# Cross-attention with a quantised feed-forward: another order of work in the prologue and the query phase

## The reference

```python
def attn(Q, K, V, WQ, WK, WV, WO, mask):          # 16 heads of 64
    Qh, Kh, Vh = (einsum('btd,hdk->bhtk', a, w) for a, w in ((Q, WQ), (K, WK), (V, WV)))
    logits = einsum('bhtk,bhsk->bhts', Qh, Kh) / sqrt(64) + mask * -1e9
    A = einsum('bhts,bhsv->bhtv', softmax(logits), Vh)
    return concat_heads(A) @ WO
def ffn(x, W1, b1, W2, b2):                        # 1024 hidden, quantised with the range of the whole tensor
    return qlinear(gelu(qlinear(x, W1, b1)), W2, b2)
x = x + attn(layernorm(x), ctx, ctx, WQ, WK, WV, WO, mask)
x = x + ffn(layernorm(x), W1, b1, W2, b2)
```

## Time and profile before

| | |
|---|---|
| median of three runs | 1099.45 us (1097.84 to 1099.54) |
| the profiled execution | 1099.71 us, of which its span 1097.6 us |
| TensorE busy | 1025.7 us (93%) |
| VectorE, ScalarE, GpSimd busy | 938.5 us (85%), 855.1 us (78%), 767.9 us (70%) |
| mean granted TensorE clock | 0.991 of full speed |
| first query product of TensorE | 19.47 us after the span's start |
| first key product | 98.08 us |

### The profile page before, as it was taken

The page is one execution under the profiler, slowest core; times in us unless marked ns, Lnnn a source line. Parts: engine busy times, 40 slices in busy tenths (PEclk is TensorE's granted clock), DMA queues, the critical chain, the costliest instruction groups (busy, mean ns, idle before and its releaser), DMA issues.

```text
span 1097.6 us, 37623 instructions
## 1 busy us (share of the span) xinstructions
PE 1025.7 (93%) x10639; PEld 643.8 (59%) x10639; DVE 938.5 (85%) x2668; ACT 855.1 (78%) x1809; POOL 767.9 (70%) x1106
## 2 busy tenths in 40 slices
PE   3999999999999999999999999999999999997728
PEld 2555566666666666666666666666666666665317
DVE  5776888888888888888888888888888888886997
ACT  3665888888888888888888888888888888886906
POOL 2337777777777777777777777777777777774800
PEclk9999999999999999999999999999999999999969
DMA  8400776666666666666666666666666666664003
GB/s 243 132 1 14 133 134 134 135 138 138 138 138 138 134 134 134 137 138 135 134 135 136 135 134 135 136 138 134 132 134 136 138 138 135 134 134 140 1 0 120
DMA packets 435436, 136.75 MB, mean 125 GB/s; under 512 B 407666, under 2 KB 434390, under 8 KB 435414
## 3 DMA queue, kind: packets, MB, share of 16 engines
q1 hardware_dynamic: 435414, 136.47, 59.5%
HBM read 28.60 MB, written 6.55 MB: 32 GB/s over the span
## 4 chain that ended last, share of the span: by engine, by line
PE 64%; DVE 13%; issue 10%; ACT 9%; DVEq 2%; DMA 2%; ACTq 1%; POOL 1%; SPq 0%; POOLq 0%
PE front L368 16%; PE front L370 14%; PE front L369 14%; PE back L1309 8%; PE front L1287 5%; PE tp L1287 4%; ACT prob L742 3%; DVE k_l L1039 3%; DVE hrange L1138 3%; DVE hrange L1139 3%; DVE prob L985 2%; ACT q_h L796 2%; ACT k_h L752 1%; DVEq L374 1%; ACT ctx_h L792 1%
## 5 line engine op out<-in xcount | busy, mean ns | idle before, releaser
L616 POOL TENSOR_TENSOR hl<-prob,hl 100x361 f16<-100x361 f32 x511 | 430.7, 855 | 67.7 <-ACT hl L748 39.9
L742 ACT ACTIVATE prob<-prob,nmax 100x361 f32<-100x361 f32 x512 | 293.9, 587 | 39.0 <-DVE nmax L985 38.9
L1309 PEld LDWEIGHTS back<-v,pT 128*128 128x128 f16 (+1 forms) x4608 | 163.9, 97 | 39.7 <-issue 9.3
L748 ACT ACTIVATE hl<-prob 100x361 f16<-100x361 f32 x352 | 176.1, 500 | 7.9
L1039 DVE SCALAR_TENSOR_TENSOR k_l<-front,k_h 128x362 f16<-128x362 f32 x256 | 136.3, 532 | 48.1 <-ACT k_h L752 45.5
L1309 PE MATMUL back<-v,pT 128*128 128x65 f16 (+1 forms) x4608 | 172.8, 193 | 1.4 <-DMA pT<-hl 1.4
L368 PE MATMUL front<-ctx_h,wk_h 128*128 128x362 f16 x512 | 164.3, 321 | 5.4 <-issue 0.8
L370 PE MATMUL front<-ctx_h,wk_l 128*128 128x362 f16 x512 | 161.8, 316 | 0.0
L369 PE MATMUL front<-ctx_l,wk_h 128*128 128x362 f16 x512 | 161.5, 315 | 0.0
L756 ACT ACTIVATE v<-front 128x512 f16<-128x512 f32 (+1 forms) x192 | 113.9, 594 | 52.6 <-PE front L370 52.6
L368 PE MATMUL front<-wv_h,ctx_h 128*128 128x512 f16 (+1 forms) x384 | 146.3, 381 | 9.3 <-DVE k_l L1039 9.3
(11 more groups left out here) (206 smaller groups left out, 2047.6 us busy)
## 6 DMA issues: line engine op xcount, KB each, us to landing
ctx_raw<-ctxT SPq DMA_DIRECT2D x33, 361.0 KB, 3.1
pT<-hl SPq DMA_TRANSPOSE x253, 3.6
xs<-x SPq DMA_DIRECT2D x8, 400.0 KB
q_all<-x SPq DMA_DIRECT2D x32, 100.0 KB
out<-q_all SPq DMA_DIRECT2D x32, 100.0 KB
xb<-out SPq DMA_DIRECT2D x5, 640.0 KB, 8.3
out<-xb SPq DMA_DIRECT2D x25, 128.0 KB, 1.8
q_all<-wq SPq DMA_DIRECT2D x1, 1024.0 KB, 6.5
```

The lines of the kernel that those rows point to most:

```text
L616: pool.tensor_tensor(hl[0:T, n % RT, 1, 0:S], prob[0:T, n % RP, 0:S], hl[0:T, n % RT, 0, 0:S], ALU.subtract).then_inc(s_lo, 1)
L742: act.activation(prob[0:T, n % RP, 0:S], prob[0:T, n % RP, 0:S], ACT.Exp, bias=nmax[0:T, n:n + 1], scale=-1.0).then_inc(s_exp, 1)
L748: act.activation(hl[0:T, h % RT, 0, 0:S], prob[0:T, h % RP, 0:S], ACT.Copy).then_inc(s_ha, 1)
L1309: ins = pe.matmul(obank[j % 2][:, n % GH * DV:(n % GH + 1) * DV], pT[0:r, n % RT, part_ * ST + st, :], v2[half][0:r, st, v, n % HT, :], st ...
```

## The change

The change has four parts.

1. **Moments.** For chunks 0 and 1 VectorE uses one aggregate instruction per item and two small steps (`pair_x`) in place of the eight steps of `ln_moments`; for chunk 1 this work moves from GpSimd to VectorE.
2. **Prologue order.** VectorE takes the maxima of weight 0 before the statistics of chunk 1, which now stand behind `x_low(0, 0)` and `low_w(0, 0)`; the statistics of chunk 2 move into chunk 0. ScalarE's `norm_x(1, 1)` moves from the prologue to a place behind the first copy of chunk 0. TensorE multiplies the fp16 identity with itself, in two halves of 64 columns, 120 times from the start and 36 times behind the transposes of chunk 0 (`warm_up`); `top_w(0)` now stands before these transposes. The first two query tiles are made in another order: all eight products that need only the weights' high part first, then the four with the low part (`first_two`).
3. **ScalarE in each chunk.** The second half of `high_w` stands behind the second copy, before `x_high`. `norm_x` of the chunk after next is cut in two halves, one before and one after the last copy.
4. **First keys.** TensorE's wait for both banks and for the zeroed pads goes. The first two jobs of the first turn wait for the last copy of their own bank, and the wait for the pads stands before the first product of queries and keys (QP).

```diff
--- before.py
+++ after.py
@@ -203,6 +203,7 @@
     stats = place("stats", [P, B, 6], F32)
     mean = place("mean", [P, B], F32)
     var = place("var", [P, B], F32)
+    pair = place("pair", [P, 2 * TB, 2], F32)
     rstd = place("rstd", [P, B], F32)
     shift = place("shift", [P, B], F32)
     lnt = place("lnt", [P, 4, B], F32)
@@ -564,8 +565,8 @@
         link = chain(pool, s_lp)
         for c in range(NB):
             bs = slice(c * TB, (c + 1) * TB)
-            if c == 0:
-                pool.wait_ge(s_lv, 8)
+            if c < 2:
+                pool.wait_ge(s_lv, (TB + 2) * (c + 1))
             else:
                 pool.wait_ge(s_st, TB * (c + 1))
                 ln_moments(link, pool, c)
@@ -683,14 +684,15 @@
             act.activation(part_w((wq_h, wk_h, wv_h, wo_h)[n], n, half), part_w(raws[n], n, half), ACT.Identity,
                            scale=winv[:, n:n + 1]).then_inc(s_whi, 1)
 
-        def norm_x(c, par):
+        def norm_x(c, par, items=range(TB)):
 
             act.wait_ge(s_rs, c + 1)
-            for i in range(TB):
+            for i in items:
                 b = c * TB + i
                 ins = act.activation(xn[0:T, par, i, :], xs[0:T, b, :], ACT.Identity, scale=rstd[0:T, b:b + 1],
                                      bias=shift[0:T, b:b + 1])
-            ins.then_inc(s_xn, 1)
+            if items[-1] == TB - 1:
+                ins.then_inc(s_xn, 1)
 
         def x_high(c, par):
 
@@ -706,25 +708,28 @@
         def q_chunk(c, par, more=True):
             split = (c - 1 if 2 <= c <= 4 else None)
             q_out(c, 0)
+            if c == 0:
+                norm_x(1, 1)
             if split:
                 high_w(split, 0)
             q_out(c, 2)
+            if split:
+                high_w(split, 1)
             if more:
                 x_high(c + 1, 1 - par)
             q_out(c, 4)
             if c + 2 < NB:
-                norm_x(c + 2, par)
+                norm_x(c + 2, par, range(TB // 2))
             if c == NB - 2:
                 act.wait_ge(s_msk, 16)
                 act.activation(mask_b[0:T, 0:S], mask_b[0:T, 0:S], ACT.Copy, scale=-1.0e9).then_inc(s_mb, 1)
-            if split:
-                high_w(split, 1)
             q_out(c, 6)
+            if c + 2 < NB:
+                norm_x(c + 2, par, range(TB // 2, TB))
         norm_x(0, 0)
         x_high(0, 0)
         high_w(0, 0)
         high_w(0, 1)
-        norm_x(1, 1)
         for c in range(NB - 1):
             if c == NB - 2:
                 act.wait_ge(s_wlo, 8)
@@ -912,6 +917,8 @@
         def q_chunk(c, par, more=2):
 
             q_out(c, 1)
+            if c == 0:
+                stats_x(2)
             if c < 3:
                 abs_w(c + 1, 0)
             elif c < 6:
@@ -948,18 +955,26 @@
                 ctx_unit(0)
                 dve.scalar_tensor_tensor(out=wconst[:, 1:2], in0=wunit[:, 2:3], scalar=1.0 / VS, in1=wunit[:, 3:4],
                                          op0=ALU.mult, op1=ALU.mult).then_inc(s_wc, 1)
+        def pair_x(c):
+
+            bs = slice(c * TB, (c + 1) * TB)
+            dve.wait_ge(s_st, TB * (c + 1))
+            for b in range(c * TB, (c + 1) * TB):
+                dve.bn_aggr(pair[0:T, b, :], stats[0:T, b, :]).then_inc(s_lv, 1)
+            dve.wait_ge(s_lv, (TB + 2) * c + TB)
+            dve.tensor_scalar(var[0:T, bs], pair[0:T, bs, 1], EPS, None, ALU.add).then_inc(s_lv, 1)
+            dve.tensor_scalar(mean[0:T, bs], pair[0:T, bs, 0], -1.0, None, ALU.mult).then_inc(s_lv, 1)
         stats_x(0)
-        dve.wait_ge(s_st, TB)
-        ln_moments(chain(dve, s_lv), dve, 0)
-        stats_x(1)
+        pair_x(0)
         abs_w(0, 0)
         abs_w(0, 1)
         unit_w(0)
-        low_w(0, 0)
         start(dve, (s_k, s_v, s_cm, s_cr, s_sv, s_max, s_mg, s_hv, s_ri, s_nrm, s_x1, s_ln))
         x_low(0, 0)
+        low_w(0, 0)
+        stats_x(1)
+        pair_x(1)
         low_w(0, 1)
-        stats_x(2)
         for c in range(NB):
             if c == NB - 2:
                 dve.wait_ge(s_wlo, 8)
@@ -1212,8 +1227,25 @@
             wait(pe, s_cm, a + 1)
             pe.transpose(ps[:, 512 - P:512], cmax[:, 0:1].broadcast_to([P, P]), ident[:, :]).then_inc(s_ct, 1)
 
+        def first_two():
+
+            pe.wait_ge(s_whi, 1)
+            for m in range(2):
+                for k in range(KD):
+                    for t, x_ in enumerate((xnT_h, xnT_l)):
+                        pe.matmul(proj[m][:, 0:TW], wq_h[:, k, m * P:(m + 1) * P], x_[:, 0, k, :],
+                                  start=k == 0 and t == 0, stop=False)
+            pe.wait_ge(s_wlo, 1)
+            for m in range(2):
+                for k in range(KD):
+                    ins = pe.matmul(proj[m][:, 0:TW], wq_l[:, k, m * P:(m + 1) * P], xnT_h[:, 0, k, :],
+                                    start=False, stop=k == KD - 1)
+                ins.then_inc(s_qp, 1)
+
         def q_chunk(c, par, more=True):
             wait(pe, s_xtl, KD * (c + 1))
+            if c == 0:
+                first_two()
             for m in range(NM):
                 if m == NM // 2 and more:
                     x_transposes(c + 1, 1 - par)
@@ -1224,21 +1256,29 @@
                 if m == NM // 2 and c == NB - 1:
                     top_f()
                 wait(pe, s_qe[m % 2], NM // 2 * c + m // 2)
-                if c == 0 and m % (NM // 2) == 0:
-                    pe.wait_ge(s_wlo, m // (NM // 2) + 1)
+                if c == 0 and m < 2:
+                    continue
+                if c == 0 and m == NM // 2:
+                    pe.wait_ge(s_wlo, 2)
                 for k in range(KD):
                     ms = slice(m * P, (m + 1) * P)
                     ins = split3(pe, proj[m % 2][:, 0:TW], (wq_h[:, k, ms], wq_l[:, k, ms]),
                                  (xnT_h[:, par, k, :], xnT_l[:, par, k, :]), k == 0, k == KD - 1)
                 ins.then_inc(s_qp, 1)
+        def warm_up(times):
+
+            for _ in range(times):
+                for h in range(2):
+                    pe.matmul(tp[1][h * DK:(h + 1) * DK, 0:T], identb[:, h * DK:(h + 1) * DK], identb[:, 0:T],
+                              start=True, stop=True)
+
+        warm_up(120)
+        top_w(0)
         x_transposes(0, 0)
-        top_w(0)
+        warm_up(36)
         for c in range(NB):
             q_chunk(c, c % 2, c < NB - 1)
 
-
-        phase1_over(pe)
-        wait(pe, s_zero, PADS)
 
         def bank_read(kind, n, a):
 
@@ -1257,6 +1297,8 @@
                 a, ps = b + later, banks.get((kind, n))
                 if ps is not None:
                     g = jobs.index((kind, n, later))
+                    if part == "first" and g < 2:
+                        wait(pe, s_qe[g], NB * NM // 2)
                     if g >= 2 or part != "first":
                         had = (before + jobs)[g]
                         bank_read(had[0], had[1], b + had[2])
@@ -1277,6 +1319,8 @@
                                      (wv_h[:, k, hs], wv_l[:, k, hs]), k == 0, k == KD - 1)
                     ins.then_inc(s_vp, 1)
                 elif kind == "QP":
+                    if part == "first" and n == 0:
+                        wait(pe, s_zero, PADS)
                     if n % (NP_ // 2) == 0:
                         wait(pe, s_q, 2 * a + n // (NP_ // 2) + 1)
                     wait(pe, s_k, NP_ * a + n + 1)
```

## The result

The changed kernel takes 1092.83 us (median of 5 runs, 1091.09 to 1094.62); the kernel before takes 1098.49 beside it (5 runs, 1097.84 to 1099.54). The ratio is 0.9948, with a 95% interval of 0.9933 to 0.9963: faster by 5.7 us.

What follows compares the result with a forecast made beforehand. Bounds: the first 20 us, where TensorE waits behind VectorE's order and starts at half clock, and gaps in the query phase. Terms 4.5+2.6+0.7 = 7.8 us, taken from the profiled 1099.71, gave 1091.9; range 1090.3 to 1096.5.

Steps and rivals of the forecast that it cites:

- the item loop starts less than 7 us earlier: Sign, at the loop behind the query phase, that would show the prediction wrong.
- The pair's price: Prologue: two identity products on the two column halves cost 60 ns at full clock, between 44 and 88.
- one after the other: Rival, prologue: column halves do not run together; top_w(0) at 14.8, gain 4.2 us, 1095.5; chance 0.14.
- The narrow loads: Rival, prologue: each narrow load also waits for the product before it; 172 ns a pair, 1105.6 us; chance 0.06.
- The estimate made from this rule, 190 ns: Identity pair's cost by the skill's load-overlap rule, result over 1105; the prediction held that the trace disagrees.
- The first term: Prologue up to chunk 1's transposes: they begin at 21.15 instead of 25.66, 4.5 us gained.
- the hole before m=3: Chunk 0: TensorE stands still some 2.5 us; VectorE's queued work holds m=3 until about 19.4.
- GpSimd and ScalarE's start 1.35 later at 19.05: Chunk 1's normalisation: after VectorE's moments end at 17.7, norm_x(1) starts at 19.05 and takes 2.07 us.
- The second term: Query phase: ScalarE's new order removes its stops at chunk starts 3 to 5, 2.6 us gained.
- the new waits for VectorE: Query phase: VectorE's q_out copies then hold TensorE 0.25 us in chunks 3 and 4, 0.33 before chunk 5.
- The third: First keys: K0 starts 0.93 us earlier, but K2 near 99.7 instead of 100.40; 0.7 us gained.
- The clock: Rival: identity products do not raise it, 1097.3 us, or it falls in chunk 0's hole, 1094.0; chance 0.11.

Runs made afterwards that it cites:

- e7: Changed kernel with both products of each identity pair on the same column half of the array: 1096.14 us.
- e4: Changed kernel with VectorE's second low_w of weight 0 moved behind the statistics of chunk 2: 1091.98 us.
- e2: Changed kernel with only ScalarE's order in a chunk put back as in the kernel before: 1096.03 us.
- e12: The changed kernel run again without any edit: 1094.19 us, ratio 0.9954 to the kernel before.
- e11: Changed kernel with the first two query tiles made in the old order, the first product waiting for low_w(0, 0): 1093.03 us.
- e3: Changed kernel with TensorE's wait for both banks and the pads put back ahead of the first keys: 1094.85 us.
- e1: Changed kernel with all identity products (120 and 36 pairs) left out: 1091.57 us, ratio 0.9933 to the kernel before.
- e8: Changed kernel with VectorE taking chunk 1's statistics ahead of the maxima of weight 0 again: 1094.11 us.
- e10: Changed kernel with 100 identity pairs instead of 120 ahead of top_w(0): 1091.7 us.
- e5: Changed kernel with the transfers from x chunk 1 on held until wq has landed: 1090.41 us, ratio 0.9926 to the kernel before.

## Why the prediction was right, and where it was not

**The forecast**, 1091.9 in a range of 1090.3 to 1096.5, stands beside 1092.83. It made the sum against the profiled execution: 1099.71 less 7.8. There the change is 7.45 (1092.26), of which the marks explain 6.85. By the medians it is 5.7, and the number came closer than the sum did: the level that it counts from, 1099.71, is 1.2 above the median of 1098.49, and from that median a gain of 7.8 would have given 1090.7, 2.1 below the measured time. So a part of the near hit is luck. By its own sign, "the item loop starts less than 7 us earlier", it stands on the edge: K0 comes 7.08 earlier, K2 6.85.

**The pair's price** was the least certain number, and the row halves were the right neighbour. The prediction took 60 ns a pair at full clock. Measured is 44, and the 120 pairs end at 10.38 instead of 11.1 (220 products in 7.27 us, a stop of 0.45, 20 in 0.63). e7 shows the rival "one after the other": top_w(0) starts at 15.25, where that rival's working says 14.8. Its ratio to the kernel before is 0.9978, 2.4 us instead of 4.2. At chunk 1's transposes it is 1.5 later than that working (26.27 against 24.8), 0.45 of it from top_w(0) and 0.96 from GpSimd's long step (below).

**The narrow loads** are hidden: two loads and two products pass in 44 ns. The Trainium skill lists, in TensorE: Matmul & The Clock Gate, section "The mechanism", that loads overlap running products only when their row group differs. The estimate made from this rule, 190 ns, is off by more than four times here; the measurement decides. The same section also lets a load run ahead when it goes to the background weight buffer; the prediction left this out, and it is what the 44 ns agree with, though no run here shows that buffer.

**The first term** was 4.5 and is 3.37; it is the term that was mis-sized. The order of events was as predicted: maxima, top_w at 11.27 (11.1 forecast), first product at 14.65 (14.4), the hole before m=3, released by VectorE (19.52; 19.4 forecast), and the transposes behind norm_x. The failed step is "GpSimd and ScalarE's start 1.35 later at 19.05". It took 2.31 (17.86 to 20.17), because low_w, which I had myself put beside it on VectorE, stops GpSimd. The trace before had shown it: the small steps of `ln_moments` are 0.2 us long, but single ones last 1.0 to 1.2 where low_w runs beside them (1.22 at 60.40 and 1.04 at 70.12, low_w from 60.28 and 69.81). The Trainium skill says it in SBUF — State Buffer, section "SBUF: two separate sides": VectorE and GpSimd share one pair of ports, and a VectorE instruction with two inputs in SBUF, if it starts first, holds it for its whole length against a GpSimd instruction that reads SBUF. e4 agrees in both directions, with 1.02 for the step that no longer meets low_w and 1.17 for the one that now does. That top_w(0) came as forecast is luck of two errors that cancel: the forecast had it wait for the identity products until 11.1, with the maxima done at 10.4; in the run the maxima began 0.8 later than assumed and ended at 11.22, and the identity products were done at 10.38, so top_w(0) waited 0.89 us for VectorE.

**The second term** (2.6 forecast) is 2.77, and 2.81 in e2; the new waits for VectorE came as named, 0.28 in chunk 3. **The third** (0.7) is 0.71, in both comparisons, K0 by 0.94.

**The clock** was a rival at 0.11, with 2.1 us if it falls in the hole of chunk 0. Its 1097.3 for a clock that never rises has no working; its own terms, 3.8 and 2.1 later, give 1097.8. The fall in the hole happens in some executions: 2.9 us in the profile of e12, 1.7 in that of e11. The mean granted clock of the five first runs points the same way, though only one has a profile: 0.991 for 1091.09 and 1092.26, 0.987 for 1092.83, 1093.94 and 1094.62. In e3 it separates two groups 2.2 us apart. In e12 it is less clean: 0.987 for 1094.43, but 0.989 to 0.991 for the four others, 1093.25 to 1094.3. How much of the spread of 3.5 us is this fall therefore stays open; that it happens and what it costs is shown by two profiles. By this the chance given was too low.

**Identity products and first_two** I took to be part of what makes the first term. e1 and e11 show that they are not, in this kernel. Of the 3.37 us of the prologue, VectorE's order carries 1.9 at chunk 1's transposes (e8). The rest was not split: the aggregates in place of the eight steps, and the other moves, were not tried alone. What the clock gives (0.75 us at best) is used up, in most of the profiles, by the stop behind the 220th product or by a fall of the clock before the next products.

## What to carry to other kernels

Follow a shortened chain to the next thing behind it on the same engine: here 4.8 us at the first product became 3.4 at the next chunk, because the work that was moved away now stood behind, and because low_w beside it held GpSimd for 0.96. Before an instruction with two SBUF inputs is put on VectorE, look at what GpSimd does at that time. Work whose only purpose is TensorE's clock has to be measured by leaving it out: if TensorE then stands idle again before the real products, or stops on the way, it buys nothing.

## What the runs showed of the hardware

- Products on two column halves run together like those on two row halves: 36 pairs of 64-column loads and 100 columns in 1.78 us, drain included, 3.21 at half clock. On one and the same half they take 3.37 at full clock (e7).
- GpSimd's instructions wait while VectorE runs an instruction with two SBUF operands: 1.02 becomes 1.99, 0.20 becomes 1.17. Beside VectorE's maxima, which read one operand, its steps keep their 0.2 (0.21 at 20.85 in the changed kernel, maxima from 20.69 to 21.89).
- A burst of 240 straight-line products stopped after the 220th for 0.45 to 2.0 us in nine of ten profiles (TensorE idle, put down to issue); in the tenth (e11) it did not stop, and neither did a burst of 200 (e10). The cause is open.
- The clock fell in one of two profiled executions of the same program, with TensorE busy 2.27 us in a stretch of 5 (2.36 in the one where it stayed up), and came back 5.7 us after the transposes began again. In e11 it fell with 3.03 us busy in the same stretch and came back after 3.4. So the busy time in this hole alone did not decide.
- At the start the clock came up at different times for the same products: between 5.0 and 5.5 us the records hold 32 identity products in e5, 24 in e10 and 18 in the changed kernel, where 32 in half a microsecond are reached only from 7.0 on.
